# Delta attention with sums picked into rows and its Exp one step later; feature attention with joint numerators and sums

## What is computed

```python
# layer 1 attention (16 key heads, 32 value heads, sequences of 64 steps)
q, k, v = split(silu(conv4(x @ W_qkvz)))        # z goes past the convolution
g = -exp(A_log) * softplus(a + dt_bias); alpha = exp(g)
q = l2norm(q) * DK ** -0.5; k = l2norm(k)       # eps 1e-6
def step(S, inp):
    S = S * alpha; err = S^T k; S = S + k (v - err) * beta; return S, S^T q
og = o * silu(z)
og = og * rsqrt(mean(og * og) + EPS) * norm_weight
return og @ W_out

# layer 3 cross attention, over features (heads of 8 features)
qk = einsum('bdm,bdn->bmn', qh, kh) / sqrt(8)
sm = softmax(qk, axis=-1)
ret = einsum('bmn,bcn->bcm', sm, vh)
```

## Time and profile before

| | us |
|---|---|
| median of 3 runs | 5372.94 (5361.59 to 5376.61) |
| the profiled execution | 5364.03 |
| its span | 5362.3 |
| busy PE / PE weight loads | 4880.0 / 3163.8 |
| busy DVE | 3129.6 |
| busy ACT | 2001.2 |
| busy POOL | 860.8 |

### The profile page before, as it was taken

How to read it: one execution, slowest core, us unless ns; L and a number is a source line. 1 busy time by engine, 2 the same in 40 slices (tenths; PEclk the granted TensorE clock), 3 DMA queues, 4 the chain that set the end, 5 groups by cost and what they waited for, 6 DMA issues and landing times. The chain is left out here.

```text
span 5362.3 us, 88025 instructions
## 1 busy us (share of the span) xinstructions
PE 4880.0 (91%) x35704; PEld 3163.8 (59%) x35704; DVE 3129.6 (58%) x5675; ACT 2001.2 (37%) x2716; POOL 860.8 (16%) x1240
## 2 busy tenths in 40 slices
PE   8349998799999999999888999995999998899899
PEld 5235555466666666667455777774555554455555
DVE  7862223778888888884543666666222226666433
ACT  3211111556565665663233555553111111333311
POOL 3310000235253353532110000000000002100000
PEclk8569999799999999999789999996999998799899
DMA  2114442121212212111100000000444431000143
GB/s 62 31 36 128 126 128 84 42 64 50 61 46 54 57 50 61 46 51 27 50 29 20 17 12 17 12 1 27 128 128 127 128 120 32 33 25 25 42 131 119
DMA packets 386221, 325.25 MB, mean 61 GB/s; under 512 B 238915, under 2 KB 281416, under 8 KB 384766
## 3 DMA queue, kind: packets, MB, share of 16 engines
q1 hardware_dynamic: 385822, 319.64, 20.8%
HBM read 284.54 MB, written 30.63 MB: 59 GB/s over the span
## 5 line engine op out<-in xcount | busy, mean ns | idle before, releaser
L673 DVE TENSOR_TENSOR f_act_g<-f_act_g,f_pu 128x512 f32<-128x512 f32 x288 | 198.1, 688 | 1037.2 <-ACT f_act_g L607 1037.2
L607 ACT ACTIVATE f_act_g<-f_pg 128x512 f32<-128x512 f32 x288 | 171.9, 597 | 1290.3 <-PE f_pu L555 1290.3
L2989 DVE SCALAR_TENSOR_TENSOR g_y<-a_f,a_cw,g_y 128x504 f32<-128x504 f32 x714 | 490.1, 728 | 212.3 <-ACT g_y L2850 206.5
L572 PE MATMUL f_py<-f_w_out,f_hidden 128*128 128x256 f32 x2304 | 550.1, 382 | 18.8 <-DVE f_hidden L678 18.8
L572 PEld LDWEIGHTS f_py<-f_w_out,f_hidden 128*128 128x128 f32 x2304 | 440.5, 191 | 201.5 <-issue 155.7
L555 PE MATMUL f_pg<-g_xT,f_w_in 128*128 128x512 f32 x1152 | 550.0, 600 | 0.0
L555 PE MATMUL f_pu<-g_xT,f_w_in 128*128 128x512 f32 x1152 | 543.5, 594 | 0.0
L3152 PE MATMUL a_f<-g_xT,a_w 128*128 128x512 f32 x952 | 448.1, 615 | 20.9 <-DVE g_y L2989 14.7
L555 PEld LDWEIGHTS f_pu<-g_xT,f_w_in 128*128 128x128 f32 x1152 | 220.3, 191 | 278.4 <-issue 278.4
L3152 PEld LDWEIGHTS a_f<-g_xT,a_w 128*128 128x128 f32 x952 | 181.1, 196 | 232.9 <-issue 222.6
L555 PEld LDWEIGHTS f_pg<-g_xT,f_w_in 128*128 128x128 f32 x1152 | 221.5, 193 | 157.2 <-issue 142.6
(11 more groups left out here) (500 smaller groups left out, 8724.6 us busy)
## 6 DMA issues: line engine op xcount, KB each, us to landing
f_w_in<-in_f_in_w SPq DMA_DIRECT2D x288, 256.0 KB, 2.9
f_w_out<-in_f_out_w SPq DMA_DIRECT2D x288, 128.0 KB, 2.0
f_scale<-f_comb SPq DMA_DIRECT2D x280, 128.0 KB, 3.1
f_scale<-f_comb SPq DMA_DIRECT2D x76, 256.0 KB, 3.4
a_c_row<-c_rows SPq DMA_DIRECT2D x128, 128.0 KB, 3.1
a_w<-in_a_w SPq DMA_DIRECT2D x16, 512.0 KB, 3.6
n_blocks<-a_N SPq DMA_DIRECT2D x256, 32.0 KB, 1.7
a_Nd<-n_blocks SPq DMA_DIRECT2D x64, 128.0 KB, 2.3
```

What stands on the lines that cost most here:

```text
L572: last = pe.matmul(py[b % 2][:, t, :], hidden[u][:, t * P:(t + 1) * P], w_out[v][:, :], start=(j == 0 and t % 2 == 0), stop=(j == FT - 1), ...
L673: dve.tensor_tensor(act_g[u][:, :], act_g[u][:, :], pu[u][:, :], ALU.mult).then_inc(gated, 1)
L2989: last = dve.scalar_tensor_tensor(out, v3(front(n, j)[:, :], SEQ)[:, :, 0:SEQ - back_by], cw[(n // NBLK) % 2][:, j, TAPS - 1 - back_by:TAP ...
```

## The change

In stage a1:

- The squares of q and of k are both taken by ACT (`square_conv`, 128 x 1024 in place of 128 x 512) and put after `silu_z`, not before it.
- Their sums: eight matmuls with 32-column weights `pick` and the squares as moving data put the sums in rows (`norm_sums`), ACT copies the rows out (`keep_norms`), PE transposes them (`turn_norms`), ACT adds epsilon (`take_norms`). DVE's four instructions for this (L2973, L2978, L2980, L2981) go.
- The same for the sum of squares of the gated output: `sum_squares`, `keep_sums` on ACT, `turn_squares` on PE.
- `merge_left` makes only the 32 columns that are used.
- The clamp of the decays goes from DVE's minimum to ACT's Relu (with the sign of `gap` turned), and clamp and Exp of block k-1 stand in ACT's step k, behind `keep_m` and among the norms, where Exp of block k stood at the end of step k. DVE's `decays(new)` stays at the head of its step, with its wait.

In stage x3: the pattern of v carries ones in the columns between, so that one matmul gives numerators and sums (`attend` makes half as many), the sums are brought to their heads' rows by two matmuls (`trade_sums`), the maxima are turned by 2 matmuls in place of 32 into a bank of their own, and DVE adds a `join`.

The core of the diff:

```diff
@@ stage a1, ACT
+                def keep_norms(n):
+                    act.wait_ge(z["norm_summed"], n + 1)
+                    act.copy(norm_rows[:, :], eb[:, 0:P]).then_inc(z["norm_rows_kept"], 1)
+                def take_norms(n):
+                    act.wait_ge(z["normed"], n + 1)
+                    act.activation(ss[:, n % STATS, 0, :].rearrange("p (w t) -> p t w", w=2), by_group(eb[:, P:2 * P]), ACT.Identity,
+                                   bias=EPS).then_inc(z["norm_taken"], 1)
+                def clamp(n):
+                    act.wait_ge(z["apart"], n + 1)
+                    act.activation(gap[:, :, :], gap[:, :, :], ACT.Relu).then_inc(z["clamped"], 1)
                 def decay(n):
-                    act.wait_ge(z["decayed"], n + 1)
+                    act.wait_ge(z["clamped"], n + 1)
                     if n:
                         act.wait_ge(z["a_ready"], n)
-                    act.activation(E[:, :, :], gap[:, :, :], ACT.Exp).then_inc(z["exped"], 1)
+                    act.activation(E[:, :, :], gap[:, :, :], ACT.Exp, scale=-1.0).then_inc(z["exped"], 1)
...
                     if is_block(back):
                         keep_m(back)
+                    if is_block(turn):
+                        keep_norms(turn)
+                        clamp(turn)
+                        take_norms(turn)
+                        decay(turn)
                     if is_block(merge):
                         keep_yb(merge)
...
                     if is_block(back):
+                        keep_sums(back)
                         root_o(back)
                     if is_block(new):
-                        decay(new)
                         silu_conv(new)
                         silu_z(merge)
+                        square_conv(new)
@@ stage a1, DVE
                     if n:
                         dve.wait_ge(z["exped"], n)
-                    dve.tensor_tensor(gap[:, :, :], c_row[n % 2][:, :, :], of_block(c_all, n), ALU.subtract).then_inc(z["apart"], 1)
-                    dve.wait_ge(z["apart"], n + 1)
-                    dve.tensor_scalar(gap[:, :, :], gap[:, :, :], 0.0, None, ALU.min).then_inc(z["decayed"], 1)
+                    dve.tensor_tensor(gap[:, :, :], of_block(c_all, n), c_row[n % 2][:, :, :], ALU.subtract).then_inc(z["apart"], 1)
@@ stage a1, PE
-                    for t in range(TPB):
-                        last = pe.matmul(eb[:, t:t + 1], sq[:, t * P:(t + 1) * P], one[:, :], start=True, stop=True)
-                    last.then_inc(z["normed"], 1)
+                    for w_ in range(2):
+                        for t in range(TPB):
+                            last = pe.matmul(eb[group[t], 0:P], pick[:, w_, :], sq[:, w_, t * P:(t + 1) * P],
+                                             start=(w_ == 0), stop=(w_ == 1), skip_group_check=True)
+                    last.then_inc(z["norm_summed"], 1)
+                def turn_norms(n):
+                    pe.wait_ge(z["norm_rows_kept"], n + 1)
+                    pe.transpose(eb[:, P:2 * P], norm_rows[:, :], G.ident[:, :]).then_inc(z["normed"], 1)
...
                         key_products(turn)
+                        turn_norms(turn)
...
                         sum_squares(back)
                         project_y(back, 0)
+                        turn_squares(back)
@@ stage x3, PE
-                    for j in range(GR):
-                        for c in range(KC):
-                            for g in range(GR):
-                                last = pe.matmul(pM[quad[g], j * D + c * P:j * D + (c + 1) * P],
-                                                 mx[:, c, g, j:j + 1].to_broadcast([P, 32]), minus[:, :], start=True, stop=True)
+                    if t >= 2:
+                        pe.wait_ge(z["inverted"], 2 * (t - 1))
+                    for c in range(KC):
+                        last = pe.matmul(pM[:, c * P:(c + 1) * P], mx[:, c, :, :].rearrange("p g e -> p (g e)"), minus[:, :],
+                                         start=True, stop=True)
```

More of the change, by code:

```diff
@@ L2014, in feature_attention @@
         quad = [slice(32 * g, 32 * g + 32) for g in range(GR)]
-        parts = [(c, half) for c in range(KC) for half in range(2)]
+        parts = [(c, half) for half in range(2) for c in range(KC)]
         with nc.Block() as block:
@@ L2184, in attend, with trade_sums @@
                             pe.wait_ge(z["evicted"], t)
[L2185 to L2191, removed]
+                    j = 2 * half + b
+                    for g in range(GR):
+                        at = g * GR * WIDE + j * 32
+                        last = pe.matmul(pO[quad[g], half * D:(half + 1) * D], vz[t % 2][:, c, at:at + 32], prob[k][:, g, b, :],
+                                         start=(c == 0 and b == 0), stop=(c == KC - 1 and b == 1))
+                    if b:
+                        last.then_inc(z["attended"], 1)
+                def trade_sums(t):
+                    pe.wait_ge(z["evicted"], t + 1)
+                    if t:
+                        pe.wait_ge(z["inverted"], 2 * t)
+                    for half in range(2):
+                        last = pe.matmul(pD, trade[:, half, :], both_of[:, half * D:(half + 1) * D], start=(half == 0), stop=(half == 1))
+                    last.then_inc(z["traded"], 1)
                 pe.wait_ge(z["set_up"], 2)
-                pe.wait_ge(z["s_here"], 32)
+                pe.wait_ge(z["s_here"], 48)
                 for i in range(UNITS):
@@ L3103, in _ @@
                         decays(0)
-                    take_norms(k - TURN)
                     norms(k - TURN)
@@ L3238, in sum_squares, with turn_squares @@
                         pe.wait_ge(z["x_ready"], n + BACK - MERGE + 1)
-                    for t in range(TPB):
-                        for h in range(2):
-                            j = 2 * t + h
-                            last = pe.matmul(eb[:, j:j + 1], osq[:, h, t * P:(t + 1) * P], one[:, :], start=True, stop=True)
+                    if n:
+                        pe.wait_ge(z["var_ready"], n)
+                    for h in range(2):
+                        for t in range(TPB):
+                            last = pe.matmul(eb[group[t], AT_YB:AT_YB + P], pick[:, h, :], osq[:, h, t * P:(t + 1) * P],
+                                             start=(h == 0), stop=(h == 1), skip_group_check=True)
                     last.then_inc(z["ssq_made"], 1)
+                def turn_squares(n):
+                    pe.wait_ge(z["sum_rows_kept"], n + 1)
+                    pe.transpose(eb[:, AT_YB + P:AT_YB + 2 * P], sum_rows[:, :], G.ident[:, :]).then_inc(z["ssq_turned"], 1)
                 def project_y(n, two):
```

180 lines of the change are left out of this document (101 added, 79 removed).

## The result

| | before, us | after, us |
|---|---|---|
| median of 4 runs each | 5374.77 (5361.59 to 5382.93) | 5683.91 (5673.13 to 5686.61) |
| the profiled execution | 5364.03 | 5685.43 |
| its span | 5362.3 | 5683.4 |
| mean granted clock of PE | 0.927 | 0.883 |

The kernel became slower: the ratio is 1.0578, with a 95% interval of 1.056 to 1.0595. Forecast were 5600 us (5425 to 5690).

What follows compares the result with a forecast made beforehand. The prediction took PE to bound the kernel before, at 23.9 us per a1 step, with DVE and ACT about as long. Profiled 5364 + 286 (a1 steps) - 19 (fill) - 11 (drain) - 20 (x3) = 5600 us, range 5425 to 5690.

Steps and rivals of the forecast that it cites:

- the forecast's own case: Whole run: a1 steps of 29.2 us with PE's clock falling, 5600 us (5545 to 5675), chance 0.6.
- The wait that decides: a1, head of DVE's step: `decays(new)` waits 3 to 5 us for ACT's Exp, delaying the add that `outputs` needs.
- The ring at full clock: a1: the closed loop of waits through DVE, ACT and PE takes 26.7 us a step, against 23.9 before.
- The clock: a1: PE's clock falls in its gap; `outputs` takes 3.4 us, the projection 1.1 more; step 29.2 us, +286 us over 54.
- Fill and drain: a1's first seven steps and its last eight without projections: -19 us and -11 us.
- PE's own work: a1: PE's work in a step falls from 23.9 to 21.9 us.
- x3: Stage x3: -3.2 us per tile, -48 us over 15 tiles at full clock, about -20 us taken.
- the fifth of the time at the lower level: Stage x3: a fifth of the time at PE's low clock, where a whole tile would take 6.3 us more.
- The table load: a1, ACT before Exp: counted as 1.28 us; by the skill page's 2.66 per switch, 28.1 us a step, 76 us more.
- the ring without the clock: Rival for a1: PE keeps full speed over the gap, steps of 26.7 us, 5437 us in all; chance 0.2.
- PE stays the bound: Rival for a1: Exp ends before DVE needs `gap`, steps fall to 21.9 us, 5178 us in all; chance 0.07.
- x3 loses its clock: Rival for stage x3: low PE clock there gives +95 us in place of -20, 5715 us in all; chance 0.1.

Runs made afterwards that it cites:

- PE kept busy: The changed kernel with 10 unused matmuls added in PE's gap, ahead of `merge_right`: 5522.58 us, ratio 1.0294 to before (with 20 of them 5739.01 us).
- two-buffer kernel: The changed kernel with two buffers for `gap`, so DVE's subtraction of block k waits for the Exp of block k-2: 5236.97 us, ratio 0.9757 to before.
- the Exp put back: The changed kernel with Relu and Exp of block k back at the end of ACT's step k, one buffer: 5348.04 us, ratio 0.9958 to before.
- the Exp moved with two buffers: The kernel before with only the Exp a step later on ACT and two buffers for `gap`: 5353.80 us, ratio 0.9971 to before.
- run 161: Not a label but a time, 161 us faster than after: the changed kernel with 10 unused matmuls in PE's gap, 5522.58 us.

## Why the prediction was right, and where it was short

The direction and the cause held. The loss was put at +236 us and came out at +321 on the profiled execution (+309 between the medians). The range held by luck: 5684 us lies 6 us under its upper end, above the 5675 of the forecast's own case, and x3, which gained 18 us more than forecast by two errors that met, kept it inside. By its steps:

- *The wait that decides.* Right. DVE waits before L3029 for the Exp in every step, and PE before `outputs` for DVE's add, the two places named. The wait of DVE was put at 3 to 5 us and is 6.89. The clock is not why, as it is 6.88 with PE kept busy. The prediction's own terms give it: 8.9 us from the Silu to the end of Exp, less some 2 for `scales` and the adds that DVE does meanwhile. The two-buffer kernel shows that this wait is the whole of the loss.
- *The ring at full clock.* Counted as 26.7, measured as 27.06 with PE kept busy. From the Silu to the end of Exp I had counted 26.6 - 17.7 = 8.9 us; the trace has 1539.63 to 1548.5, 8.9. From the Exp to the end of the add, 6.5; the trace has 6.6.
- *The clock.* This is **the term that was mis-sized**. I took it to fall in the gap, which it does. I gave `outputs` 3.4 us and it has 3.61 from start to start. I took 1.1 us more for the projection behind it, between bounds of 0 and 2.4, "since outputs are part of the recovery". They shorten it little: the clock stays down for 3.9 us of the projection, which takes 5.55 from start to start in place of 3.6, +1.95, near the upper bound. Together the clock costs 3.6 us and not 2.55. The row nearest to the case was the projection after a wait of 3.43, and it should have stood as it was. Add the 0.36 that the ring itself is longer (0.26 of them a wait of 0.56 for the sums, where I allowed 0.3), and the step is 30.66, not 29.2, just over the upper bound of 30.6: 54 x 1.46 = 79 us. What else was off nearly cancels, and the sum was missed by 85.
- *Fill and drain.* Forecast -19 and -11. Where the fourth fetch of weights starts, the fill is 16.6 us ahead of before, but at the subtraction of block 10 only 5.4: the steps between, which start the ring, were not counted. From the last `gap` to the stage's end it takes 179.3 us after 182.2, only -3.
- *PE's own work.* Forecast 21.9, measured 22.14. The sums by rows take 0.57 us plus 0.11 for the transpose, as counted (0.5 and 0.12).
- *x3.* Forecast -20, measured -38 in the trace, by two errors that met. A tile takes 19.48 us after 21.74, a gain of 2.3 and not 3.2:

```profile
5159.28 0.71 PE L2192 MATMUL x_pMD<-x_minus,x_mx 128*128 128x128 f32 x4 [0.43 <-DVE x_mx L2095]
...
5178.76 0.71 PE L2192 MATMUL x_pMD<-x_minus,x_mx 128*128 128x128 f32 x4 [0.43 <-DVE x_mx L2095]
```

  The turned maxima take 0.64 us before the next matmul, not the 0.4 that I had, and `trade_sums` takes 1.07, not 0.45. The other error is the clock: it is 0.97 in the stage with the change, as it was before (0.97 in 4680 to 4983 us), so the fifth of the time at the lower level did not come:

```profile
5045.00:5318.00 273.00, 253.06 (x2311) 124.95 (x2311) 195.92 (x329) 125.53 (x139) 16.73 (x41) 0.97 0.08 24
```

- *The table load.* An Exp starts 0.01 us after its load of 1.28 ends, 0.02 in the earlier trace rows. The Trainium skill's page ScalarE: Activation LUTs (section "What ACT_TABLE_LOAD costs") adds a drain of 1.38 us to each switch. By that rule the ring at full clock would be 28.1 us, an estimate. It measured 27.06, and its pieces on ACT add up without a drain, so the traces here decide against it.

The rivals: *the ring without the clock* fell by the clock of 0.83, though its step is what the kernel with PE kept busy shows. *PE stays the bound* fell for this kernel, and is what a second buffer makes of it: 5237 us, where the rival had 5178, with 54 steps of 22.4 to 22.6 instead of 21.9 and a smaller gain in x3. *x3 loses its clock* fell.

One thing stays open: which gap brings the clock down. The length of the last wait does not decide it alone. With two buffers, a wait of 0.28 us in each step, no projection is slow between 1300 and 2300 us. After a wait of 4.91 the clock falls in every step. With the Exp put back the same wait of 1.0 us stands before `outputs` in every step, and six steps of about 42 in that stretch are slow. In the one shown above PE was busy again when the clock fell, 1 us behind the wait, and it stayed at 0.50 for 7 us. The clock fell also 2.8 us behind a wait of 0.15 (the Exp moved with two buffers, granted clock 0.99), for 3.3 us. So single slow steps come with short waits too; what a long gap does is to bring one every time.

## What to carry to other kernels

When an operation is moved in one engine's list, look for who waits on the buffer that it frees, and what stands behind that wait in the other engine's list: a single buffer written at the head of one list and read in the middle of another ties the whole step into one ring, and a second buffer, or writing it later in the list, opens it. When a ring puts a gap of several microseconds into PE's list, price the matmuls behind the gap by the slow rows that the trace already has, whole, and for all of them up to the next that runs at full speed. And measure an order of the list together with the buffer it needs: in the changed kernel the later Exp cost 336 us with one buffer and gained 111 with two.

## What the runs showed that I had not expected

- The fall of the clock costs much beside the gap itself: behind 4.9 us of idle time, 5.55 us of matmuls take 9.16. Ten useless matmuls of 4.5 us in the gap made the whole run 161 us faster.
- The move of the Exp without the rest of the change is worse than with it (5833 against 5684 us), since one more small DVE instruction, `take_norms`, stands behind the wait and stops PE before three groups of small matmuls. They run at the low clock ahead of `outputs`, which starts 2.4 us later behind the subtraction than in after.
- The Exp between root and Silu costs 1.3 us per step as soon as PE is not the bound. In the trace of before the same delay was there, 1550.63 - 1549.80 = 0.8 us, and PE's load hid it.
